# The order of full and half expert blocks: one half block ahead of each pair, six full blocks at the end

## The reference

```python
logits = x @ router_weight                       # 8 experts
probs = softmax(logits); top_p, top_i = top_k(probs, 2)
top_p = top_p / sum(top_p)
# rows are sorted by expert; each expert has cap rows at most, later ones are dropped
fc1 = gelu(einsum('ech,ehf->ecf', xt, moe_w1))   # 256 -> 512
fc2 = einsum('ecf,efh->ech', fc1, moe_w2)        # 512 -> 256
moe_out = zeros.at[padded_tid].add(fc2 * padded_probs)
return h1 + moe_out
```

## Time and profile before

| | |
|---|---|
| runs | 1173.57 us median of 3 (1173.4, 1173.57, 1183.42) |
| profiled execution | 1186.0 us, of which the span is 1184.2 |
| TensorE busy (matmuls) | 1096.5 us, 93% of the span |
| TensorE weight loads | 1001.6 us, 85% |
| VectorE busy | 919.2 us, 78% |
| ScalarE busy | 812.6 us, 69% |
| GpSimd busy | 547.8 us, 46% |
| moved by DMA | 171.79 MB, 145 GB/s over the span |

### The profile page before, as it was taken

How to read it: one execution, slowest core, us unless ns; L and a number is a source line. 1 busy time by engine, 2 the same in 40 slices (tenths; PEclk the granted TensorE clock), 3 DMA queues, 4 the chain that set the end, 5 groups by cost and what they waited for, 6 DMA issues and landing times. The chain is left out here.

```text
span 1184.2 us, 24751 instructions
## 1 busy us (share of the span) xinstructions
PE 1096.5 (93%) x8034; PEld 1001.6 (85%) x8036; DVE 919.2 (78%) x2290; ACT 812.6 (69%) x1840; POOL 547.8 (46%) x504
## 2 busy tenths in 40 slices
PE   6899999999999889989889888899999999999993
PEld 4699999999999777877777776789889889989983
DVE  5657787777877589998999987987777787777771
ACT  1447777767776578887888887557676667766770
POOL 0012121221222233477877766788645555554556
PEclk9889999999999999999999999999999999999997
DMA  8423353443431212344544475678777677676754
GB/s 294 119 73 100 113 160 114 126 148 112 136 91 61 89 45 92 100 145 146 154 142 140 142 220 190 167 188 227 161 196 196 158 177 199 178 170 172 189 127 46
DMA packets 119016, 171.79 MB, mean 145 GB/s; under 512 B 14508, under 2 KB 90188, under 8 KB 118860
## 3 DMA queue, kind: packets, MB, share of 16 engines
q1 hardware_dynamic: 92300, 136.00, 37.0%
q0 software_dynamic: 26592, 34.24, 15.4%
HBM read 104.04 MB, written 67.97 MB: 145 GB/s over the span
## 5 line engine op out<-in xcount | busy, mean ns | idle before, releaser
L1447 POOL DMA_INDIRECT out_rows<-y,row x142 | 235.0, 1655 | 177.9 <-DVE y L2051 91.9
L179 PE MATMUL gh<-w2h,hh 128*128 128x256 f32 x568 | 160.7, 283 | 1.1 <-issue 1.1
L181 PE MATMUL gh<-w2h,hl 128*128 128x256 f32 x568 | 160.7, 283 | 0.0
L180 PE MATMUL gh<-w2l,hh 128*128 128x256 f32 x568 | 160.7, 283 | 0.0
L1982 DVE TENSOR_TENSOR hl<-h,hh 128x512 fp32r<-128x512 f32 (+1 forms) x156 | 99.2, 642 | 76.7 <-ACT h L1653 73.3
L1652 ACT ACTIVATE hh<-gw 128x512 fp32r<-128x512 f32 (+1 forms) x78 | 44.0, 564 | 128.2 <-issue 126.4
L1425 POOL DMA_INDIRECT slot_rows<-kept,slot x104 | 111.1, 1068 | 28.7 <-issue 28.7
L179 PEld LDWEIGHTS gh<-w2h,hh 128*128 128x128 f32 x568 | 108.9, 192 | 2.4 <-issue 1.2
L180 PEld LDWEIGHTS gh<-w2l,hh 128*128 128x128 f32 x568 | 108.9, 192 | 1.2
L181 PEld LDWEIGHTS gh<-w2h,hl 128*128 128x128 f32 x568 | 108.9, 192 | 0.0
L937 POOL TENSOR_TENSOR layer_low<-whole,layer_high 128x528 fp32r<-128x528 f32 x32 | 41.7, 1325 | 135.1 <-ACT layer_high L855 135.1
(11 more groups left out here) (375 smaller groups left out, 3908.8 us busy)
## 6 DMA issues: line engine op xcount, KB each, us to landing
w1e<-in_moe_w SPq DMA_DIRECT2D x39, 512.0 KB, 6.1
w2e<-in_moe_w SPq DMA_DIRECT2D x39, 512.0 KB
xr<-slot_rows SPq DMA_DIRECT2D x32, 532.0 KB, 5.8
xg<-x_rows SPq DMA_DIRECT2D x62, 260.0 KB
x_rows<-x SPq DMA_DIRECT2D x32, 264.0 KB, 2.9
xT<-in_xT SPq DMA_DIRECT2D x32, 256.0 KB, 2.7
x<-in_x SPq DMA_DIRECT2D x32, 256.0 KB, 3.7
out_rows<-res SPq DMA_DIRECT2D x64, 128.0 KB, 2.6
```

The lines of the kernel that those rows point to most:

```text
L179: nc.tensor.matmul(out, at_a(ah), at_b(bh), start=first, stop=False, skip_group_check=True)
L180: nc.tensor.matmul(out, at_a(ah), at_b(bl), start=False, stop=False, skip_group_check=True)
L181: return nc.tensor.matmul(out, at_a(al), at_b(bh), start=False, stop=last, skip_group_check=True)
L1447: g.indirect_dma_start(out=out, out_offset=bass.IndirectOffsetOnAxis(ap=row[m % NR][:, t:t + 1], axis=0), in_=y[m % 2][:, t, :], in_offset ...
```

## The change

The seven H now stand ahead of a pair of F each, and the six F that are left follow one another at the end. H moves to places 12, 15, 18, 21, 24, 27 and 30; places 33 to 38 are F. The indices keep their order among F and among H, so each block has the same rows and expert as before; the table on the core is not touched, nor the code of any engine.

```diff
 ORDER = list(range(EARLY))
+PAIRS = 2
 for _half in range(HALVES):
-    ORDER += [FULLS + _half] + list(range(len(ORDER) - _half, EARLY + (_half + 1) * (FULLS - EARLY) // HALVES))
+    ORDER += [FULLS + _half] + list(range(EARLY + PAIRS * _half, EARLY + PAIRS * (_half + 1)))
+ORDER += list(range(EARLY + PAIRS * HALVES, FULLS))
```

## The result

The changed kernel took **1185.76 us**, median of 20 runs (1179.91 to 1191.69). The kernel before, run beside it, took 1178.62 us, median of 20 (1171.03 to 1190.11), so its own median came out 5 us higher than in the three runs known at first. The ratio of the runs is 1.0066, 95% interval 1.0039 to 1.0093: about 7 to 8 us slower, within 1%. Of the 20 runs of before, 9 took 1171 to 1174.7 us; of the 20 of after, none took less than 1179.9.

What follows compares the result with a forecast made beforehand. The prediction took GpSimd's scatter chain to set the end, TensorE's chain how early that can be. Its scatter sums gave +3.5 and +2.3 us, including TensorE's delay; it forecast +3, so 1173.57 + 3 = 1176.5 us, range 1169 to 1187.

Steps and rivals of the forecast that it cites:

- TensorE's path: TensorE in the expert stage: shorter turns behind H cover less of the wait for xTe, ending +1.5 us later, bounds 0 to 1.7.
- Moved DMAs: Each block's loads (w1, w2, x) move with it on SP's queue: 0 us for the loads themselves.
- The scatter chain: GpSimd's scatters and their landings, about a block behind, set the end: +3.5 us by one sum, +2.3 by another.
- The first sum: Scatter chain from block 15's start: six groups at 32.4 us, three F, then the last three; end 1187.7, +3.5 us.
- The second sum: Scatter chain from TensorE's T(36), start of its pass 36: then 10.2 + 10.2 + 29.9, end 1186.5, +2.3 us.
- T(36) + 0: Block 34's scatters were taken to start right at T(36), when TensorE turns block 38, at 1136.25 us.
- GpSimd 10.2 to 10.9, so it gains on TensorE: In the six F before the end, GpSimd takes 10.2 to 10.9 us a block against TensorE's 11.93.
- rival 1: Scatters catch up in the six F at the end: priced -3.5 us, 1170, floor 1162; chance 0.18.
- GpSimd runs without a pause of its own, about one block behind: In the expert stage, GpSimd's idle time ahead of a block is the landing of the block before, shown as 3.1 to 6.9 us.
- Rival 2: Scatter chain becomes the pace in groups H F F, places 15 to 32: up to +20.9 us, 1194.5; beyond 1%: 0.05.
- Rival 3: The order does nothing, end within 1 us: 1173.6; held inside the forecast's bounds, which together have chance 0.62.
- The rest: Chance 0.15 for a median up to 10 us higher for reasons not the order's, or something no row shows.

Runs made afterwards that it cites:

- late_before: The kernel before with twelve fills on GpSimd ahead of block 8's scatters, making the scatter chain late: 1181.3 us, ratio 1.0042.
- late_after: The changed kernel with twelve fills on GpSimd ahead of block 8's scatters: 1186.21 us, ratio 1.0088 to the kernel before.
- shift2_before: The kernel before with two more indirect DMAs into a spare tensor, issued far ahead on GpSimd: 1179.84 us, ratio 1.0023.
- half_end: The changed kernel with its last H moved from place 30 to 38: 1184.19 us, ratio 1.0035 to the kernel before.
- pairs_late: The changed order with the run of six F ahead of the pairs, H at 18, 21, ..., 36: 1171.63 us, ratio 0.9961 to the kernel before.
- shift2_half_last: The kernel before's H F F F groups with H at 14, 18, ..., 38, plus two more indirect DMAs far ahead on GpSimd: 1184.76 us, ratio 1.0079.
- pairs_half_last: The order with the run of six F ahead of the pairs, its last H moved from place 36 to 38: 1177.95 us, ratio 1.0033 to the kernel before.
- pad64_after: The changed kernel with 64 semaphore increments at the start of GpSimd's program: 1183.25 us, ratio 1.0052 to the kernel before.

## Why the prediction was right, and where it was not

**TensorE's path, +1.5 us, bounds 0 to 1.7**: right. It measured +1.6 without scatters and +2.1 in the pair of profiles. The seven waits for xTe, six with the short turn behind them and one without, came as described. About half of the 0.4 above the upper bound is in the second wait with scatters: three of the six were 0.87 to 0.90 us in place of 0.71, while two of before's were 0.53 in place of 0.37.

**Moved DMAs, 0**: the loads themselves cost TensorE nothing in after, whose only waits are the two kinds above. Their effect on landings was left to the next sum, and was more than that sum held.

**The scatter chain, +3.5 or +2.3**: this is the term that was too small; from T(12) to the end it came to +5.7. The first sum comes near by luck up to block 33: block 15 started 9.3 us earlier behind T(12) than it had it, since the chain was ahead, and the six groups took 203.2 us and not 194.4, one of them 41.45 with the pause in it and the last 34.79 (the groups up to block 23 took 31.3 to 31.7, the one from block 27 32.17). From block 33 on it is 2.7 us short. The tail of 23.8 us is just above the 20 to 23 that the prediction named as a sign of being right. The second sum shows where, step by step. T(36) lies 259.70 us behind T(12), foreseen 259.10: +0.6. "T(36) + 0" was wrong: block 34 started 1133.35 - 1131.75 = 1.6 us behind T(36). And the blocks from 34 on took 1184.8 - 1133.35 = 51.45 us, foreseen 50.3: +1.15. Together 3.4 us more than 2.3. The step that failed is "GpSimd 10.2 to 10.9, so it gains on TensorE". In the run of F, blocks 32 and 33 took 1120.95 - 1108.29 = 12.66 and 1133.35 - 1120.95 = 12.40 us, with an idle time of 5.3 to 5.4 for the landing, because each landing met the next block's loads. The landings of block 33 and of block 34 in after, in the columns of the earlier trace rows:

```profile
1128.04:1132.48 4.44, 4.44 (x42) 4.44 (x41) 4.36 (x7) 2.36 (x5) 0.00 (x0) 1.00 0.82 178
1141.12:1143.23 2.11, 2.11 (x20) 2.11 (x19) 2.11 (x3) 1.20 (x3) 0.00 (x0) 1.00 0.54 62
```

With 178 GB/s in all under way the landing took 4.44 us from the end of the last issue, with 62 GB/s it took 2.11. Only from block 34 on, with the loads done, did a block take 10.1 to 10.75 us. The prediction had seen 11.9 for early F blocks and had held it against rival 1, but had not put it into its own sum.

The Trainium skill ("DMA: Bandwidth & Descriptors", "Anatomy of one DMA — SWDGE (gpsimd) path") gave an estimate of 2.3 us for a scatter to land. The idle time of 3.0 to 3.1 us that the prediction held against it is not the landing alone. In after, the scatters from 1140 us on land 3.8 us after the start of their issue (median of 17), of which 1.54 are the issue. Counted from the issue's end that is 2.3 us, and so the trace agrees where little else moves; counted from its start it doesn't. The other 0.8 us of the idle time lie between the landing and the next issue. Beside loads the idle time was 4.1 to 6.6 us, so the trace doesn't agree where it mattered here.

**"GpSimd runs without a pause of its own, about one block behind"**: a description of one profile, taken for the kernel. The sum compared a late chain with a late chain, and for that case the record gives 4.9 us (late_before to late_after, medians) and 5.7 (the pair of profiles). The 7.1 (medians) or 7.8 us (ratio, interval 4.6 to 11.0) measured hold these two. **What was not in the sum is that the old order's chain can also end ahead, which the new one's did in no profile.** Against a chain that ends ahead, as in `shift2_before`, the change costs 9 to 11 us from T(10) on; against one that ends behind, 4 to 7 (last column of the table). A mixture of both would give the 7 to 8 measured. How many of before's own runs end ahead is not shown: its only profile was behind, and the run times can't tell.

**Rival 1** (the scatters catch up in the six F): no. Not in six and not in the ten of `half_end`. Its floor, 1172.8 - 1164.0 = 8.8 us of tail, was not reached in any profile either: the least is 12.5 in `pairs_late`, whose chain was never behind, because the last block's scatters still waited 3.08 us for the landing of the block ahead. **Rival 2** (the scatter chain becomes the pace): not in after, whose y waits for GpSimd only 1.01 us at the most before the last blocks and hold nothing. Where the chain is behind and the pause comes on top, it does: TensorE waited 3.59 us in one place in `shift2_half_last`, and 0.8 in `late_after`. **Rival 3** (the order does nothing): no. **The rest** ("a median may fall 10 us higher for reasons that are not the order's") took part: 5 us of the 12 between forecast base and result are the median of before itself, 1173.57 in three runs and 1178.62 in twenty. Of the result's distance to the forecast, 9 us, 5 come from there and 4 from the change itself, +7 and not +3. That the result lies inside the range is owed to its upper edge of 1187, next to the 1186.5 that it gave for such a shift of the median; the forecast's own bounds, a change of 0 to 6 us, were passed. So far it is luck.

## What to carry to other kernels

A chain that runs behind the busiest engine without holding it can have two states at the same pace, and only its place at the end counts. Look for both before reading one profile, and sum a change for either. The spread of the run times won't show them where earlier stages vary more than the states differ (here 20 us against 5); mark a point up to which all versions do the same work, and compare profiles from there. Cost a landing beside the loads that it will meet, not by its best row. The order whose chain stayed ahead in its profile had the lowest median, 1171.6 us; that its late H are the reason is not shown, since moving one of them two places further gave 1178.0 with a chain that had fallen behind earlier.

## What the runs showed of the hardware

- GpSimd stood still for 4.9 to 6.2 us, with no releaser in the trace, ahead of the 93rd scatter-add of the chain, in every trace in which that scatter was not the first of its block. In `pairs_late`, where it was the first, GpSimd stood still for 5.33 us too, while its y had been done for 1.5 us and the block ahead had landed 3.1 us before. Neither 64 more instructions at the start, nor 12 fills with their waits inside the chain, nor two more indirect DMAs ahead moved it to another scatter. At the 29th, 64 earlier and always first in its block, three traces have 2.4 to 4.5 us of idle time without a releaser (before, `pairs_late`, `pairs_half_last`), the others 0.3 to 1.1, or 3.54 beside a landing (`shift2_half_last`). One trace (`pad64_after`) has a further such pause of 5.55 us ahead of its 111th. What GpSimd does in that time stays open.
- GpSimd's idle time for the landing of a full block's scatters of 128 KB each was 3.0 to 8.0 us in the rows shown. From the end of the last issue it took 2.11 us with 62 GB/s under way and 4.44 with 178 (after, blocks 34 and 33). At one and the same place (ahead of block 9, behind the same order) the idle time was 4.87 us in one trace and 8.00 in another.
- TensorE's granted clock was 1.00 from T(10) to TensorE's end in 13 of the 14 profiles. In `shift2_half_last` it was 0.71 from 1040 to 1050 us, when TensorE had stood still for 3.59 us; the pass took 18.96 us and not 12.51.
